# The last thirteen groups of each graph layer: rows copied a group ahead, and the third layer's norm and attention table made inside them

## The reference

```python
def _conv(x, row, col, edge_type, edge_weight, W, b):
    deg = segment_sum(ones, col)
    norm = deg**-0.5[row] * deg**-0.5[col] * edge_weight
    xw = einsum('ni,tio->tno', x, W)            # four tables, one per edge type
    x_j = xw[edge_type, col] * norm[:, None]
    return leaky_relu(segment_sum(x_j, row) + b, 0.01)
z1 = _conv(x, ..., W1, b1); z2 = _conv(z1, ..., W2, b2); z3 = _conv(z2, ..., W3, b3)
x = layernorm(x + (x + z1 + z2 + z3) / 4)
xp = (x * (x != 0)) @ W                        # two heads of 64
a_src, a_dst = per-head dot products of xp with att_src, att_dst
out = softmax over each node's edges of leaky_relu(a_src[src] + a_dst[dst], 0.2), times xp[src], summed
x = layernorm(x + out + bias)
```

## Time and profile before

| what | us |
|---|---|
| median of three runs | 9099.33 |
| lowest, highest | 9099.24, 9101.07 |
| the profiled execution | 9109.24 |
| its span, first to last instruction | 9107.4 |

### The profile page before, as it was taken

The page is one execution under the profiler, slowest core; times in us unless marked ns, Lnnn a source line. Parts: engine busy times, 40 slices in busy tenths (PEclk is TensorE's granted clock), DMA queues, the critical chain, the costliest instruction groups (busy, mean ns, idle before and its releaser), DMA issues.

```text
span 9107.4 us, 149340 instructions
## 1 busy us (share of the span) xinstructions
PE 5676.2 (62%) x32763; PEld 4294.9 (47%) x32764; DVE 4601.6 (51%) x12830; ACT 3980.5 (44%) x12251; POOL 6423.1 (71%) x6527
## 2 busy tenths in 40 slices
PE   4885555555555555555556555555654777777775
PEld 3664444444443444444443444444443666666665
DVE  9994232323233232322323232232325999999998
ACT  5552232323233232322323232232324888888887
POOL 0566777777775777777775777777775777777775
PEclk9996555555556555555556555555555787777876
DMA  1001111111123111111112111111111434343333
GB/s 50 32 35 54 53 53 53 53 53 53 53 67 79 53 53 53 53 53 53 53 53 90 53 53 53 53 53 53 53 53 57 117 114 116 115 115 115 115 115 94
DMA packets 432675, 612.43 MB, mean 67 GB/s; under 512 B 232026, under 2 KB 249479, under 8 KB 432527
## 3 DMA queue, kind: packets, MB, share of 16 engines
q0 software_dynamic: 208832, 428.96, 16.9%
q1 hardware_dynamic: 223694, 182.02, 6.3%
HBM read 437.29 MB, written 51.28 MB: 54 GB/s over the span
## 4 chain that ended last, share of the span: by engine, by line
issue 26%; POOL 25%; DMA 23%; DVE 18%; DVEq 4%; PE 4%; ACT 1%; POOLq 0%; ACTq 0%; SPq 0%
POOL g_rows L718 24%; DMA g_rows<-gcn_table,rec_idx 22%; DVEq L1563 3%; DVE a_miss L1674 2%; DVE a_max L1679 1%; DVE state L1732 1%; DVE lo_hot L1249 1%; DVE a_lo L1758 1%; DVE acc L1738 1%; DVE v_hot L1389 1%; PE wide L1149 1%; DVE a_sum L1702 1%; DVE state L1692 1%; DVE a_drop L1720 1%; DVE a_left L1753 1%
## 5 line engine op out<-in xcount | busy, mean ns | idle before, releaser
L718 POOL DMA_INDIRECT g_rows<-gcn_table,rec_idx x4836 | 4592.4, 950 | 1644.4 <-issue 1212.7
L877 ACT ACTIVATE g_step<-g_rows,rec_w 128x128 f32 x5580 | 1781.3, 389 | 4211.5 <-POOLq L698 3921.5
L1180 PE MATMUL bank<-g_step,g_hot 128*128 128x128 f32 x7440 | 1853.4, 428 | 1646.8 <-ACT g_step L877 1533.0
L1180 PEld LDWEIGHTS bank<-g_step,g_hot 128*128 128x128 f32 x7440 | 1593.5, 316 | 2078.9 <-issue 2078.9
L1588 DVE TENSOR_TENSOR acc<-acc,bank 128x512 f32 x930 | 639.9, 688 | 2765.4 <-PE bank L1180 2761.5
L743 POOL DMA_INDIRECT a_roll<-gat_table,src_plane x1612 | 1527.0, 947 | 494.4 <-issue 444.9
L1180 PE MATMUL wide<-g_step,g_hot 128*128 128x128 f32 x3720 | 930.0, 429 | 896.9 <-ACT g_step L877 871.0
L1180 PEld LDWEIGHTS wide<-g_step,g_hot 128*128 128x128 f32 x3720 | 799.8, 317 | 1111.7 <-issue 1111.7
L930 ACT ACTIVATE a_cand<-a_miss,a_rows 128x128 f32<-128x128 bf16 x3608 | 1096.0, 386 | 19.7 <-DMA a_rows<-a_roll 19.5
L1588 DVE TENSOR_TENSOR acc<-acc,wide 128x512 f32 x465 | 320.0, 688 | 1495.8 <-PE wide L1180 1494.1
L1579 DVE TENSOR_TENSOR g_hot<-bank,rec_lo 128x512 f32<-128x512 f32 x1395 | 952.7, 683 | 3.6 <-DVE z L1608 0.3
(11 more groups left out here) (262 smaller groups left out, 5070.9 us busy)
## 6 DMA issues: line engine op xcount, KB each, us to landing
a_rows<-a_roll SPq DMA_DIRECT2D x451, 264.0 KB
g_rows<-gcn_table,rec_idx POOLq DMA_INDIRECT x4836
gcn_table<-rows SPq DMA_DIRECT2D x147, 256.0 KB, 2.0
a_roll<-gat_table,src_plane POOLq DMA_INDIRECT x1612
e_dst<-by_dst_dst SPq DMA_DIRECT2D x451, 2.0 KB
gat_table<-acc SPq DMA_DIRECT2D x7, 462.0 KB
out_x<-xs SPq DMA_DIRECT2D x6, 448.0 KB
gcn_slots<-nothing SPq DMA_DIRECT2D x4, 468.0 KB, 5.7
```

The costliest lines, as they stand in the source:

```text
L718: pool.indirect_dma_start(out=g_rows[:, tile % RING, :], out_offset=None, in_=gcn_tables[layer % 2], in_offset=bass.IndirectOffsetOnAxis(a ...
L877: last = nc.scalar.activation(g_step[:, j, k, :].unsqueeze(1), g_rows[:, bass.ds(slots[k], 1), :], ACT.Copy, scale=rec_w[:, bass.ds(q.at(0 ...
L1180: last = nc.tensor.matmul(sums_of(j)[:, bass.ds(places[k], D)], g_hot[:, j % 3, k, :], g_step[:, j % 3, k, :], start=False, stop=(k == GP ...
```

## The change

Three things, all in the last thirteen batches' groups:

1. ACT copies rows a group ahead. At group 451 it scales its own group and the next; at group 451 + n it scales group 452 + n and then makes the rows of batch n - 1. The register values are read a group earlier still, right behind the scaling (`ahead`). PE reads its values ahead too.
2. In layers 1 and 2 a batch moves one group up: PE does `products(n - 1)` and then `turn(n)` after group 451 + n (before: n - 2 and n - 1). The copy of the transposed batch moves from ACT to DVE, behind `next_z`; DVE waits there for PE's transposes.
3. In the third layer the norm and the attention table are made by batch in the same groups. The 7-block operations become 4-block ones, transposes share a bank four at a time, and the products use the three banks of the other layers.

```diff
@@ ACT, scale_rows.body
-                    scale(q)
-                    if 0 <= n < NBATCH:
-                        if n >= 2:
-                            rows_of(n - 2)
-                        if n >= 1:
-                            turn(n - 1)
+                    if n <= 0:
+                        scale(q, slots_of(q))
+                    if 0 <= n < NBATCH:
+                        following = Step(GRP, q.base + 1)
+                        scale(following, ahead.pop() if n else slots_of(following))
+                        if n + 1 < NBATCH:
+                            ahead.append(slots_of(Step(GRP, q.base + 2)))
+                    if n >= 1 and layer < 2:
+                        rows_of(n - 1)
+                    if n >= 1 and layer == 2:
+                        act.wait_ge(s_tT, turns(3, n - 1) + 1)
+                        nc.scalar.copy(*turned(n - 1)).then_inc(s_tc, 1)
+                        gat_rows(n - 1)
+                    if 0 <= n < NBATCH and layer == 2:
+                        ln_sqrt(n, BATCHES[n])
+                        act.wait_ge(s_third, n + 1)
+                        for b in BATCHES[n]:
+                            last = nc.scalar.activation(xs[:, b, :], xs[:, b, :], ACT.Identity,
+                                                        scale=mv[:, b, 1:2], bias=mv[:, b, 0:1])
+                        last.then_inc(s_added, 1)
@@ PE, sum_gcn.body
-                    add_up(q)
-                    if 0 <= n < NBATCH:
-                        if n >= 2:
-                            products(n - 2)
-                        if n >= 1:
-                            turn(n - 1)
+                    add_up(q, ahead.pop() if n >= 1 else places_of(q))
+                    if 0 <= n < NBATCH:
+                        if n >= 1 and layer < 2:
+                            products(n - 1)
+                        ahead.append(places_of(Step(GRP, q.base + 1)))
+                        if layer < 2:
+                            turn(n)
+                    if layer == 2 and n >= 1:
+                        turn(n - 1)
+                        products(n - 1)
@@ DVE, layer_gcn.body, behind the add of the group
+                        if layer == 2 and 1 <= n <= NBATCH:
+                            masked(n - 1)
                         if 0 <= n < NBATCH:
                             next_z(layer, slice(BATCHES[n].start, BATCHES[n].stop))
+                            if layer < 2:
+                                dve.wait_ge(s_tT, turns(layer + 1, n) + 1)
+                                V.tensor_copy(*turned(n)).then_inc(s_tc, 1)
+                            else:
+                                ln_stats(BATCHES[n], 16.0 * 1e-5)
+                                hot(q)
+                                third(n)
```

More of the change, by code:

```diff
@@ L419, in product_bank, with turned @@
             return bank[(1, 6, 7)[b % 3]][:, :]
+        def turned(n):
+            width = len(BATCHES[n])
+            return nodeT[:, 0:width, :].rearrange("p b e -> p (b e)"), bank[4][:, 0:width * P]
         def turns(layer, n):
@@ L832, in _, with ln_sqrt, gat_rows @@
             act.wait_ge(s_count, 9)
-            def scale_rows(layer):
[L835 to L840, removed]
+            def ln_sqrt(n, blocks):
+                cs = slice(blocks.start, blocks.stop)
+                act.wait_ge(s_ln, n + 1)
+                nc.scalar.sqrt(mv[:, cs, 1], mv[:, cs, 1]).then_inc(s_ln2, 1)
+            def gat_rows(n):
+                for b in BATCHES[n]:
+                    act.wait_ge(s_tm, 3 * NB + b + 1)
+                    nc.scalar.copy(acc[:, b, :], product_bank(b)[:, 0:GAT_W]).then_inc(s_tr, 1)
+            def scale_rows(layer):
+                ahead = []
                 def rows_of(n):
@@ L884, in _ @@
                 scale_rows(layer)
[L886 to L912, removed]
             def body(q):
@@ L976, in _ @@
                              ).then_inc(s_planned, 1)
[L978 to L994, removed]
             def count_sources():
@@ L1145, in products @@
                     pe.wait_ge(s_tc, turns(layer + 1, n) + 1)
+                    if layer == 2 and n == 0:
+                        pe.wait_ge(s_row, 1)
+                    weights = w_all[:, layer + 1, :] if layer < 2 else w_row[:, :]
                     for i, b in enumerate(BATCHES[n]):
@@ L1613, in next_z, with ln_stats @@
                     chain(V.tensor_tensor(xs[:, bs, :], xs[:, bs, :], z[:, bs, :], ALU.add))
+            def ln_stats(blocks, eps):
+                for b in blocks:
+                    last = V.bn_stats(stats[:, b, :], xs[:, b, :])
+                chain(last)
+                for b in blocks:
+                    last = V.bn_aggr(mv[:, b, :], stats[:, b, :])
+                chain(last)
+                var = mv[:, blocks.start:blocks.stop, 1]
+                chain(V.tensor_scalar(var, var, eps, None, ALU.add))
+                dve.sem_inc(s_ln, 1)
@@ L1615, in _ @@
             for layer in range(3):
                 layer_gcn(layer)
-            def ln_stats(cs, eps):
-                for b in range(cs.start, cs.stop):
-                    last = V.bn_stats(stats[:, b, :], xs[:, b, :])
-                chain(last)
-                for b in range(cs.start, cs.stop):
-                    last = V.bn_aggr(mv[:, b, :], stats[:, b, :])
-                chain(last)
-                chain(V.tensor_scalar(mv[:, cs, 1], mv[:, cs, 1], eps, None, ALU.add))
-                dve.sem_inc(s_ln, 1)
```

79 lines of the change are left out of this document (36 added, 43 removed).

## The result

The changed kernel takes 8985.2 us (median of four, 8984.2 to 8987.5) against 9099.3 beside it, 114 us less: ratio 0.9875, 95% interval 0.9857 to 0.9892. The forecast was 9017, and its range began at 8996. The direction and the three places were right, and all three gave more than was forecast.

A forecast was written before the change was run, and what follows sets the result against it. At the hand-overs a chain going round between engines was taken as the bound, no engine being full. Gains of 38, 38 and 6 us sum to 82, taking 9099.3 to 9017 us; range 8996 to 9055.

The forecast's parts named there:

- What bounds the kernel, and where the gain lies: At three hand-overs, a chain round between engines, 10.07 us a group; overlap gains 38, 38 and 6 us.
- The turn in layers 1 and 2: Last groups of layers 1 and 2: 6.1 us a group instead of 10.07, ends 5.7 and 7.3.
- ACT's 5.8: Layers 1 and 2, per group: scaling 1.3, register reads 1.3, four rows spaced 0.71, restart 0.35; sum 5.8 us.
- The round of 5.7: Layers 1 and 2: PE's sum, products, transposes, clearing and next sum in a loop with DVE's add and z, 5.7 us.
- The start, 454's sum at 2708: End of layer 1: from DVE's add at 2692.75, 453's sum ends near 2699.6 and 454's near 2708.
- The tail, 9.3 and 2.8 us: End of layer 1: 9.3 us from 463's sum through the last row, then 2.8 to POOL's first gather.
- DVE's copy at 0.69: Layers 1 and 2: copying the transposed batch takes DVE 0.69 us, against 0.58 on ACT; some 2 us in all.
- The third layer's turn, 9.0 us with ends 8.2 and 10: Third layer's last groups: 9.0 us each through PE at low clock, DVE alone 8.1 to 8.2; 6 us less.
- Rival B: Turns of 5.7 us in layers 1 and 2, high clock in the third layer: 99 us less, 9000; chance 0.13.
- A: PE's clock goes up and down inside turns of 7.3 us: 57 us less, 9042; chance 0.26.
- D: PE stays at low clock through layers 1 and 2, turns of 11.1 us: slower, 9126; chance 0.03.
- C: Loop does not open: DVE's wait and ACT's register reads fall in sequence, turns about 9.5 us: 9091; chance 0.06.

The follow-up runs named there:

- the last two kernels: Changed kernel with g_hot behind the norm's small operations, z by block, PE clearing ahead of products: 8979.6 us; the same with three xs passes off the hand-overs: 8964.6 us.
- the last kernel: Changed kernel with g_hot moved, z made by block, PE clearing ahead of products, and three xs passes off the hand-overs: 8964.6 us, ratio to before 0.9852.

## Why the prediction was wrong, step by step

- **What bounds the kernel, and where the gain lies**: right. The whole result stands at the three hand-overs, and the loop opened because PE no longer waits for `g_step` (3.27 us before, nothing now; up to 3.27 again where each group is scaled in its own turn).
- **The turn in layers 1 and 2, 6.1 us with ends 5.7 and 7.3**: the step that failed. It is 5.28, and 5.35 on the mean of the nine, below the lower end. Three sums of 5.5 (PE), 5.8 (ACT) and 5.7 (a round) were made, and then something was put on top for engines that hand work to each other. There is no such cost in it: two engines wait inside the turn, 0.85 and 0.90 us, and the third is full. PE's 5.5 was nearest; its sum overlaps the first product (0.99, not 1.0 to 1.15) and the clearing takes 0.32 from where the transposes end to the next sum, not 0.5. ACT's 5.8 counted a read of registers at 1.3 us from the bracket of the earlier trace rows. The read lasts 1.8 us there; it begins beside the copy of 0.58, and the bracket is what it sticks out. Beside the scaling of 1.27 it sticks out by some 0.6, where ACT waits for PE anyway. Where the read stands ahead of the scaling ACT is indeed the bound, at 5.68. The round of 5.7 added the same pieces with the first product behind the sum's whole length. From the sum of group 454 to that of 463 are nine turns, so this is worth 7 us at each hand-over.
- **The start, 454's sum at 2708**: mis-sized by 3 us. The changed kernel has it end at 2701.8, of which 3 us are the general lead of its execution. 453's sum came where the forecast had it (its end is 2696.2, against 2699.6 less the lead); behind it the forecast put products, clearing and sum between the two clocks (5.2 and 2.4 us), but from 2697 on PE was at the high one, and they took 3.8 and 1.5.
- **The tail, 9.3 and 2.8 us**: right, 11.9 from 463's sum to the first gather. Start and turns make the 10 us by which the idle time is shorter than the forecast 38; layer 2 has the same, 12.
- **DVE's copy at 0.69**: as estimated, and without effect on the turn; the 2 us that the dearer copy might have cost are not there, since with the copy on ACT, at 0.58, the turn is the same 5.28.
- **The third layer's turn, 9.0 us with ends 8.2 and 10**: failed as well, 8.13. DVE's sum by itself was put at 8.1 to 8.2, and that is what came. The 9.05 for PE's round took 1.3 us for the register read between ACT's scaling and its copy; in the trace the read lasts 1.1 us and runs beside the two scalings, ACT ends them at 6818.11 and then only waits for PE's transposes, so the copy ends near 2.5 us behind the start of the mask instead of 3.6. The low clock was right (0.55). Eleven turns of 0.87 less, and 0.8 less behind the last mask (4.4 us for 5.2), make the 10 us between 6 and 16.
- **Rival B** (turns of 5.7, the third layer at 8.2, 9000) was nearest. Its turn in layers 1 and 2 was still too long, and its third layer came at the low clock, not at the high one it named. A and D fall by the clock of 1.00, C by the turns.
- **The range**: its lower end was B, which held terms that were waits in the trace of before and could overlap. With turns of 5.3 and 8.1 it would have been 24 us below 9017 (nine turns of 0.8 twice, eleven of 0.9), and with both starts 3 us earlier 8987.

## What to carry to other kernels

When a loop that goes round between engines is opened, forecast the new turn by the plain sum of the fullest engine, measured from start to start where it already runs without gaps. Here nothing had to be added for the handing over in layers 1 and 2; in the third layer the turn was DVE's sum with its wait for ACT. Do not take a gap in the old trace for work of that length: a register read of 1.8 us showed as 1.3 behind a copy and costs next to nothing beside a scaling, until it gets long enough to hold up what comes next. So look at the read itself. Whether that engine is the bound is told by giving it one operation more: 0.86 us more a turn was 0.86 us, while 0.58 us more on ACT was nothing. Before an instruction is moved ahead of another, look at what is queued behind the second one on the engine that consumes it: PE's sum moved ahead of the products put a square root behind them on ACT, and DVE waited 1.46 us for it.

## What the hardware showed

- A DVE pass of 6.69 us with two inputs in SBUF holds up a gather that POOL issues during it: at all three hand-overs, before and after the change, the gather ended 0.8 us behind the pass. A memset of 5.61 us, which has no input, held up none; which property of the two makes the difference was not varied. The Trainium skill (SBUF — State Buffer, SBUF: two separate sides) describes a port pair that VectorE and GpSimd share, which one instruction keeps for its whole length; the rows agree. It was worth 15 us of this kernel, and the prediction only said that the pass moves along; the change neither won nor lost by it.
- The same kernel takes 9100 us on two chips and 12174 on a third, by gathers that take the same 0.94 us each to issue and whose tiles are freed late. Why is open.
- In the last two kernels one turn of the third layer is 8.9 instead of 7.5 us, with a wait of 1.8 us ahead of the add that the profile puts down to nothing. It is DVE's own read of registers ahead of that add, as in the turn of 5.81 us above (below, the four from 6780 to 6870):

```profile
6835.89 0.69 DVE L1583 TENSOR_TENSOR acc<-acc,bank 128x512 f32 x1 [1.77 <-issue]
L1553 DVEq TENSOR_LOAD <-gcn_at x4: 729/984/2208, 6788.3 to 6857.4; - x4
```

The long one, 2.21 us, begins at 6833.45 and ends at 6835.66; in the last kernel it is 2.26, while the four of the changed kernel in this stretch take 0.73 to 0.80. ACT reads its own registers from 6833.88 to 6836.18. Whether one read holds up the other is open.
- So a read of registers out of `gcn_at` holds ACT's or DVE's queue for 0.5 to 2.4 us here, and the same read can be short or long: ACT's take 0.8 to 2.4 us in layer 1's last groups, 0.5 to 1.2 in the third layer's.
